# The last group's routing for the second feed-forward part, moved from the end of the second attention into the feed-forward loop

## The reference, cut to what matters

```python
x = x + _L1_xattn_ref(_layernorm(x), ctx, ctx, mask, mask, mask, Wq, Wk, Wv, Wo)
x = x + _L1_ffn_ref(_layernorm(x), gate_w, w1, w3, w2, ws1, ws3, ws2)

def _L1_ffn_ref(x, ...):                      # T = 4096 tokens, D = 128, E = 8 experts of 64, K = 2, shared 128
    scores = sigmoid(xt @ gate_w)
    top_scores, top_idx = top_k(scores, K)
    top_scores = top_scores / sum(top_scores)
    dense = zeros((T, E)).at[arange(T)[:, None], top_idx].set(top_scores)
    h = silu(einsum('td,edh->teh', xt, w1)) * einsum('td,edh->teh', xt, w3)
    routed = einsum('ted,te->td', einsum('teh,ehd->ted', h, w2), dense)
    shared = silu(xt @ ws1) * (xt @ ws3) @ ws2
    return shared + routed
```

## Time and profile before

| | us |
|---|---|
| runs of the kernel, median (lowest to highest of 3) | 1221.46 (1220.59 to 1227.62) |
| the profiled execution, its own time | 1222.51 |
| span of its profile | 1220.7 |

### The profile page before, as it was taken

How to read it: one execution, slowest core, us unless ns; L and a number is a source line. 1 busy time by engine, 2 the same in 40 slices (tenths; PEclk the granted TensorE clock), 3 DMA queues, 4 the chain that set the end, 5 groups by cost and what they waited for, 6 DMA issues and landing times. The chain is left out here.

```text
span 1220.7 us, 27328 instructions
## 1 busy us (share of the span) xinstructions
PE 919.2 (75%) x10334; PEld 697.5 (57%) x10334; DVE 722.6 (59%) x1774; ACT 566.3 (46%) x928; POOL 615.9 (50%) x582
## 2 busy tenths in 40 slices
PE   3478888865676654399980378988989889995998
PEld 1357666542222221399970167877777777884565
DVE  3567766535677557255534455676667776653665
ACT  1157777756565563166650133333334343332454
POOL 1258888763777767144436834445353530111454
PEclk9998989967787877699995678999899999997999
DMA  5221222007548647777758102240422313000001
GB/s 167 75 65 55 64 76 71 8 16 277 215 187 270 274 188 263 202 212 200 203 153 320 39 25 90 93 160 24 159 90 91 112 60 141 2 2 1 19 19 35
DMA packets 112064, 144.03 MB, mean 118 GB/s; under 512 B 14325, under 2 KB 93090, under 8 KB 105794
## 3 DMA queue, kind: packets, MB, share of 16 engines
q1 hardware_dynamic: 74050, 110.81, 27.0%
q0 software_dynamic: 8192, 16.79, 4.6%
q10 hardware_dynamic: 29696, 14.68, 4.2%
HBM read 76.60 MB, written 65.40 MB: 116 GB/s over the span
## 5 line engine op out<-in xcount | busy, mean ns | idle before, releaser
L929 POOL DMA_INDIRECT fetched_a<-rows_y,chosen_row x128 | 123.0, 961 | 172.9 <-DVE att_a L822 121.2
L1486 POOL DMA_INDIRECT rows_x<-rows_r,index_r x128 | 138.2, 1079 | 67.5 <-issue 36.7
L450 POOL TENSOR_TENSOR p_lo_a<-probs_a,p_hi_a 128x1024 f16<-128x1024 f32 x64 | 136.0, 2130 | 48.6 <-ACT p_hi_a L313 48.6
L629 PEld LDWEIGHTS psum<-v_x_a,probs_a 128*128 128x128 f32 x1024 | 127.0, 200 | 3.4 <-issue 0.3
L629 PE MATMUL psum<-v_x_a,probs_a 128*128 128x65 f32 x1024 | 127.8, 280 | 0.0
L1664 POOL TENSOR_TENSOR h_lo_t<-hidden_t,h_hi_t 96x512 f16<-96x512 f32 x48 | 55.5, 1155 | 92.3 <-ACT h_hi_t L1632 92.3
L807 DVE TENSOR_REDUCE negmax_a<-psum 128x8 f32<-128x1024 f32 x64 | 78.2, 1222 | 18.8 <-PE psum L614 8.3
L312 ACT ACTIVATE probs_a<-psum 128x1024 f32<-128x1024 f32 x64 | 65.7, 1026 | 34.9 <-PE psum L170 34.9
L359 DVE TENSOR_REDUCE negmax_a<-psum 128x8 f32<-128x1024 f32 x64 | 77.8, 1216 | 5.2 <-PE psum L186 5.0
L680 PE MATMUL psum<-wo,att_t_a 128*128 128x128 f32 x512 | 63.9, 278 | 8.3 <-ACT att_t_a L741 5.8
L680 PEld LDWEIGHTS psum<-wo,att_t_a 128*128 128x128 f32 x512 | 60.6, 192 | 15.8 <-DVE comb_t L797 4.8
(11 more groups left out here) (335 smaller groups left out, 2938.1 us busy)
## 6 DMA issues: line engine op xcount, KB each, us to landing
values<-v_out_r SPq DMA_DIRECT2D x16, 1040.0 KB
v_x_a<-values SPq DMA_DIRECT2D x16, 1040.0 KB
keys<-k_out_r SPq DMA_DIRECT2D x16, 1024.0 KB
listed_t<-rows_x SPq DMA_DIRECT2D x96, 128.0 KB, 2.4
rows_y<-result_t ACTq DMA_DIRECT2D x48, 256.0 KB, 2.5
k_a_a<-keys SPq DMA_DIRECT2D x16, 512.0 KB
k_b_a<-keys SPq DMA_DIRECT2D x16, 512.0 KB
q_pad_a<-narrow_q SPq DMA_DIRECT2D x64, 64.0 KB
```

The lines of the kernel that those rows point to most:

```text
L450: nc.gpsimd.tensor_tensor(p_lo[:, s % RING0, :], probs[:, s % NPR, :], p_hi[:, s % RING0, :], ALU.subtract).then_inc(s_plo, 1)
L629: last_ = nc.tensor.matmul(PV[:, part, i * (HD + 1):(i + 1) * (HD + 1)], probs[:, s % 3, lane(part, i)], v_x[:, par, b % GB, h, :], start= ...
L929: nc.gpsimd.indirect_dma_start(fetched[:, b % NF1, k, :], None, rows_y, bass.IndirectOffsetOnAxis(ap=chosen["row"][:, b, k:k + 1], axis=0) ...
L1486: nc.gpsimd.indirect_dma_start(rows_x, bass.IndirectOffsetOnAxis(ap=index[:, g * GB + t, k:k + 1], axis=0), rows[:, g % 2, t, :, :].rearra ...
```

## The change

The routing of group 7 leaves `attention1` and is done in `ffn1`, whose first 35 units don't need it.

- Its scratch tiles and semaphores are made once for both parts, by the new `grading`. `attention1` now ends at step NP + 2, and "y", "l", "m", `statistics2`, `normal2`, `grade` and `share` are left out there for g = 7.
- In `ffn1`, DVE does the statistics and POOL the normalisation ahead of their first unit. PE transposes the rows after `down(0)` (in round n = 2), makes the logits after `down(2)` (n = 4) and transposes the shares after `down(5)` (n = 7). ACT copies the rows at n = 3, takes Exp at n = 5 and copies the shares at n = 8, each after `upper(n - 1)`. DVE makes the lower rows after unit 3, the choice after unit 5, the shares after unit 6 and the lower shares after unit 8.
- These jobs need a PSUM bank. They take bank 5, so the spread shares of the first four groups (16 products) have bank 4 alone: `up` waits there until the `weighted` before it is done. From the 17th on the two banks are used by turns again.

```diff
-        if s >= lag and (s - lag) % 8 == 0 and (s - lag) // 8 < G:
+        if s >= lag and (s - lag) % 8 == 0 and (s - lag) // 8 < G - 1:
...
-    FIRST, LAST = -18, NP + 10
+    FIRST, LAST = -18, NP + 3
...
+    SPARE = bank[5]
+    LATE = slice((G - 1) * 512, G * 512)
...
+    TWO = 4 * ROUTED
+
+    def share_bank(m):
+
+        return CB[0 if m < TWO else m % 2]
...
-                    if m >= 2:
+                    if 1 <= m <= TWO:
+                        pe.wait_ge(s_a, m)
+                    elif m == TWO + 1:
+                        pe.wait_ge(s_free, 3)
+                    elif m:
                         pe.wait_ge(s_a, m - 1)
-                    nc.tensor.matmul(CB[m % 2], w["pick"][:, k, :], comb_t[:, cols], start=True, stop=True).then_inc(s_cm, 1)
+                    nc.tensor.matmul(share_bank(m), w["pick"][:, k, :], comb_t[:, cols], start=True, stop=True).then_inc(s_cm, 1)
...
+            def rows_late():
+                pe.wait_ge(s_xhat2, G)
+                for t in range(GB):
+                    last_ = nc.tensor.transpose(SPARE[:, t * P:(t + 1) * P], xhat2[:, t, :], const["ident"][:])
+                last_.then_inc(s_full, 1)
+
+            def logits_late():
+                pe.wait_ge(s_free, 1)
...
+                    last_ = nc.tensor.matmul(o, y[1][:, tok], hi[:, :], start=False, stop=True)
+                last_.then_inc(s_full, 1)
+
+            def shares_late():
+                pe.wait_ge(s_comb, G)
...
                     down(n - 2)
+                if n == 2:
+                    rows_late()
+                if n == 4:
+                    logits_late()
+                if n == 7:
+                    shares_late()
...
                     upper(n - 1)
+                if n == 3:
+                    act.wait_ge(s_full, 1)
+                    nc.scalar.activation(y[0][:, LATE], SPARE, ACT.Copy).then_inc(s_upper, 1)
+                if n == 5:
+                    act.wait_ge(s_full, 2)
+                    nc.scalar.activation(expo[:, :, :], SPARE[:, 0:GB * E1].rearrange("p (t e) -> p t e", e=E1), ACT.Exp,
+                                         scale=-1.0).then_inc(s_free, 1)
+                if n == 8:
+                    act.wait_ge(s_full, 3)
+                    nc.scalar.activation(comb_up[:, :], SPARE[0:32, :], ACT.Copy,
+                                         scale=const["low_comb1"][:, :]).then_inc(s_upper, 1)
...
+            def grade_late():
+                dve.wait_ge(s_free, 2)
...
+            statistics_late()
             for n, (g, k) in enumerate(units):
...
                 if k == 2 and g:
                     add(g - 1)
+                if n == 3:
+                    dve.wait_ge(s_upper, 1)
+                    nc.vector.tensor_tensor(y[1][:, LATE], SPARE, y[0][:, LATE], ALU.subtract).then_inc(s_free, 1)
+                if n == 5:
+                    grade_late()
+                if n == 6:
+                    share_late()
+                if n == 8:
+                    dve.wait_ge(s_upper, 2)
+                    nc.vector.tensor_tensor(comb_t[0:32, LATE], SPARE[0:32, :], comb_up[:, :], ALU.subtract).then_inc(s_free, 1)
...
+            normal_late()
             for n, (g, k) in enumerate(units):
                 pool.wait_ge(s_wh, n + 1)
```

More of the change, by code:

```diff
@@ L548, in attention1 @@
     s_fetch, s_add, s_whole = [sem(f"fetch{n}") for n in range(NF1)], sem("add"), sem("whole")
[L550 to L557, removed]
+    tiles, (s_stats2, s_mv2, s_rstd2, s_xhat2, s_choice, s_comb) = graded
+    xhat2, stats2, meanvar2, vareps2, rstd2 = (tiles[n] for n in ("xhat2", "stats2", "meanvar2", "vareps2", "rstd2"))
+    expo, biased, top8, top, marked = (tiles[n] for n in ("expo", "biased", "top8", "top", "marked"))
+    earned, total, comb, comb_up = (tiles[n] for n in ("earned", "total", "comb", "comb_up"))
     def lane(part, i):
@@ L1670, with ffn1 @@
 WRING = 5
-def ffn1(nc, mem, bank, x_all, w, y, comb_t, out):
+def ffn1(nc, mem, bank, x_all, w, y, comb_t, out, const, graded):
     def sb(name, shape, dt=F32):
@@ L1767, in add, with after, statistics_late, share_late @@
                 nc.vector.tensor_tensor(rows, YB[g % 2], rows, ALU.add).then_inc(s_x, 1)
+            done = [1 + 8 * (G - 1)]
+            def after(instruction):
+                done[0] += 1
+                instruction.then_inc(s_choice, 1)
+                dve.wait_ge(s_choice, done[0])
+            def statistics_late():
+                for t in range(GB):
+                    b = (G - 1) * GB + t
+                    last_ = nc.vector.bn_stats(stats2[:, t, :], x_all[:, b * D:(b + 1) * D])
+                last_.then_inc(s_stats2, 1)
+                dve.wait_ge(s_stats2, G)
+                for t in range(GB):
+                    last_ = nc.vector.bn_aggr(meanvar2[:, t, :], stats2[:, t, :])
+                last_.then_inc(s_mv2, 1)
+            def grade_late():
+                dve.wait_ge(s_free, 2)
+                scores_ = biased[:, :, 0:E1]
+                after(nc.vector.tensor_single_scalar(scores_, expo[:, :, :], 1.0, ALU.add))
+                after(nc.vector.reciprocal(scores_, scores_))
+                for t in range(GB):
+                    last_ = nc.vector.max(top8[:, t, :], biased[:, t, 0:E1])
+                after(last_)
+                after(nc.vector.tensor_copy(top[:, :, 0:K1], top8[:, :, 0:K1]))
+                for t in range(GB):
+                    last_ = nc.vector.match_replace(marked[:, t, :], top[:, t, :], biased[:, t, :], 2.0 * NONE)
+                after(last_)
+            def share_late():
+                after(nc.vector.scalar_tensor_tensor(earned[:, :, :], marked[:, :, 0:E1], 1.5 * NONE, biased[:, :, 0:E1],
+                                                     ALU.is_lt, ALU.mult))
+                after(nc.vector.tensor_reduce(total[:, :], earned[:, :, :], AX.X, ALU.add))
+                after(nc.vector.reciprocal(total[:, :], total[:, :]))
+                for half in range(2):
+                    last_ = nc.vector.tensor_tensor(comb[:, :, half, 0:E1], earned[:, :, :],
+                                                    total[:, :].unsqueeze(2).broadcast_to([P, GB, E1]), ALU.mult)
+                last_.then_inc(s_comb, 1)
+            statistics_late()
             for n, (g, k) in enumerate(units):
@@ L1785, in _, with normal_late @@
         def _(pool):
+            def normal_late():
+                pool.wait_ge(s_mv2, G)
+                nc.gpsimd.tensor_tensor(vareps2[:, :], meanvar2[:, :, 1], const["eps"][:, :].broadcast_to([P, GB]),
+                                        ALU.add).then_inc(s_rstd2, 1)
+                pool.wait_ge(s_rstd2, 2 * G - 1)
+                nc.gpsimd.tensor_tensor(rstd2[:, :], vareps2[:, :], const["power"][:, :].broadcast_to([P, GB]),
+                                        ALU.pow).then_inc(s_rstd2, 1)
+                pool.wait_ge(s_rstd2, 2 * G)
+                for t in range(GB):
+                    b = (G - 1) * GB + t
+                    last_ = nc.gpsimd.tensor_scalar(xhat2[:, t, :], x_all[:, b * D:(b + 1) * D], meanvar2[:, t, 0:1],
+                                                    rstd2[:, t:t + 1], ALU.subtract, ALU.mult)
+                last_.then_inc(s_xhat2, 1)
+            normal_late()
             for n, (g, k) in enumerate(units):
@@ L1893, in program @@
         with ExitStack() as scope:
-            attention1(nc, scope, psum, x_all, const, later, lists[1], chosen, kept, last["gate"], y, comb_t)
+            attention1(nc, scope, psum, x_all, const, later, lists[1], chosen, kept, last["gate"], y, comb_t, graded)
         with ExitStack() as scope:
-            ffn1(nc, scope, bank, x_all, last, y, comb_t, out.rearrange("b s d -> s b d"))
+            ffn1(nc, scope, bank, x_all, last, y, comb_t, out.rearrange("b s d -> s b d"), const, graded)
         attending.close()
```

38 lines of the change are left out of this document (32 added, 6 removed).

## The result

| | before | after |
|---|---|---|
| median of 20 runs, us (lowest to highest) | 1224.62 (1214.0 to 1233.0) | 1213.5 (1205.08 to 1223.07) |
| profiled execution, us / span | 1222.51 / 1220.7 | 1219.53 / 1217.7 |

The ratio is 0.9906, with a 95% interval of 0.9881 to 0.9932: some 11.5 us less, a gain clear of noise and just inside the 1% that I had called the bound. 1209.0 was forecast with a range up to 1212.6, so the time lies 0.9 us above the range.

What follows compares the result with a forecast made beforehand. A serial one-engine-at-a-time chain at the border, then PE in the feed-forward loop, were taken as the bound. Removed chain -14.87, start -0.1, PE work +1.2, waits +1.3 gave -12.5 us: 1221.46 to 1209.0, range 1207.0 to 1212.6.

Steps and rivals of the forecast that it cites:

- the bound: Whole kernel: 1%, about what a measurement can tell from no change, lying at 1209.25 us, just above the forecast.
- What is removed: Between attention and feed-forward loop: the serial chain from L784's end to L797's end goes, 14.87 us; the 0.28 us hand-over stays.
- The start of the loop: Before `down(0)`: full clock from the start, but POOL's normalisation delays `w_lo(0)`; `down(0)` at 7.16 against 7.25, -0.1 us.
- PE's additions: PE in the loop: eight transposes and twelve logit products add 1.2 us, none of it hidden.
- The wait at `up(7)`: Share product of `up(7)`: PE waits 1.2 us for `weighted(6)` after ACT's table loads and DVE's choice, then 0.1 for `w_lo(5)`.
- New waits, the failed term: PE in the loop: new waits sum to 1.3 us, with none at the rows, logits or transposes of the shares.
- The sum at the full clock: Whole change: -14.87 - 0.1 + 1.2 + 1.3 = -12.5 us.
- The clock rival: After PE's wait for `w_lo(0)`: clock falls, 6.8 us at half speed, price 3.2 us, time 1212.2; chance 0.15.
- the first wait: Before `down(0)`: PE stands 2 us for `w_lo(0)`, where the clock might fall.
- The gap of 1.69 us: Ahead of 993.70 in the earlier profile: said to lie between products of 512 columns and leave the clock at full speed.
- The base: Time before the change: median 1221.46 us, from which 12.5 was taken to give 1209.0.
- Its own signs: Would show it wrong: clock 0.5 after 1119, PE waiting at logits or share transposes, longer or extra loads, a longer border.

Runs made afterwards that it cites:

- e2: Changed kernel with the four normalising instructions moved from POOL to DVE, behind DVE's second unit; loop 93.54 us.
- f3: Changed kernel with normalisation split between POOL's `w_lo`, Exp, choice and shares later, share product reading scores from PSUM; attention's last add to last add 91.92 us, ratio 0.9875.
- e5: Changed kernel again, nothing edited, clock full all the way; 94.61 us from attention's last add to the last add of all, ratio 0.9916.
- e3: Changed kernel with the chosen scores held in PSUM, so the last two share instructions have one SBUF input; loop 93.35 us.
- b2: Kernel before with seven unused 128x512 subtractions added on POOL behind the last normalisation; attention's last add to last add of all 110.52 us, 4.5 more.

## Where the prediction was right, and where it was wrong

- **What is removed**: the chain of 14.87 us went whole, the hand-over of 0.3 us stayed. Right.
- **The start of the loop**: right in mechanism and to 0.1 us. The full clock was there, and POOL's normalisation ate it. e2 and f3 confirm that this wait is POOL's order.
- **PE's additions**: 1.2 us, right. From start to start in e5 the row transposes take 0.44 us, the logits 0.31 and the share transposes 0.45.
- **The wait at `up(7)`**: 1.28 us (forecast 1.2 and 0.1 behind it). Right.
- **New waits, the failed term**: "The shares (1123.27 to 1124.37, 1.1 us with the hand-over the earlier trace rows) are made at 19.5 to 20.5, and their transposes come up at 20.6: no wait". They took 2.1 us (1138.52 to 1140.61), because I had taken their price from a place where POOL was idle and moved them beside a POOL that is busy for half of each unit. PE was there at 20.5, as forecast, and stood for 1.08 us. e3 shows the cause: with one operand in PSUM the pair takes 0.29 us and the wait is gone.
- **The sum at the full clock**: with what e5 shows, -14.87 - 0.17 (`down(0)` at 7.08, not 7.25) + 1.20 + 1.28 + 1.08 is -11.48; measured is 94.61 - 106.05 = -11.44. The wait for the shares is as large as the whole difference to the forecast of -12.5.
- **The clock rival** (0.15, priced 3.2 us) came true in half: not at the first wait (2 us) but at the second pair, for 3.4 us instead of 6.8, at 1.68 us, in two of three profiles. With it, the gain is 9.8 us, without it 11.4; the measured ratio (11.5 us, interval 8.3 to 14.6) can't tell these apart, nor from 12.5. The gap of 1.69 us that spoke against the rival didn't lie between products of 512 columns: the transposes of L674, of 128 columns, stood ahead of it.
- **The base**: "I take the median 1221.46". Three runs carried it; over 20 runs the median is 1224.62, from 1214.0 to 1233.0. Of the 4.5 us between forecast and measured time, 3.2 are the base and 1.3 the change. Neither alone leads out of the range: with the base off by 3.2 us and the change as forecast the time would be 1212.2, with the change off by 1.3 it would be 1210.3, and the range went to 1212.6. It had room for the change's unknowns and none for the base.
- **Its own signs**: two of the things that it named as showing it wrong came true, PE's wait at the transposes of the shares and, in two of three profiles, the clock at 0.5 behind them.

Open: what decides whether the clock falls. The same waits were followed by a fall in two profiles and by none in two (e5, e2), with no difference in the kernel's own timing that I could see between e5 and the two that fell.

## What to carry to other kernels

A piece of work that is moved out of a hole into a busy loop must be priced with the loop's other engines running: DVE beside POOL is not DVE alone. If one serial chain is hidden under a loop with 35 units of room, put its pieces far apart and cut the longest (f3 got 14.1 us, the change 9.8 to 11.4, where the chain was 14.87 and the slow clock behind it another 2.7 by the prediction's count). And a change of 1% needs a base of more than three runs, or a stretch of the profile that repeats, here to 0.01 us at the same clock.

## What was not expected of the hardware

- DVE's `tensor_scalar` in float32 from SBUF to SBUF stood while POOL ran, in b2 through the rest of one POOL instruction and the four that followed it closely (5.13 us for 0.17).
- POOL's power costs by the number: 1.03 us for 4 numbers a partition, 1.63 for 8, 5.44 for 32. These lie on a line of some 0.16 us for each number and 0.4 us fixed.
- The kernel before took 1194 and 1195 us in a single run on each of two chips, and 1224 and 1231 in the median of 10 and 25 runs on two others, with the same program. Whether that is the chip or the manner of running isn't shown.
